# Four fused transformer layers on one core: wider products and another order in the MLPs

## What is computed

```python
h = norm(x)                                   # rmsnorm in L0, layer norm in L1, L2, L3
h = gelu(h @ w1 + b1) @ w2 + b2               # w1 (256, 1024), w2 (1024, 256)
x = x + h                                     # in L0 added to the layer's input
```

## Time and profile before

| | |
|---|---|
| median of three runs | 943.88 us |
| the profiled execution | 942.92 us |
| its span, first to last instruction | 941.1 us |
| instructions | 16083 |
| TensorE busy | 864.7 us (92%) |
| VectorE busy | 615.5 us (65%) |
| ScalarE busy | 486.8 us (52%) |
| GpSimd busy | 483.4 us (51%) |
| mean granted TensorE clock | 0.982 of 2.4 GHz |

### The profile page before, as it was taken

The page is one execution under the profiler, slowest core; times in us unless marked ns, Lnnn a source line. Parts: engine busy times, 40 slices in busy tenths (PEclk is TensorE's granted clock), DMA queues, the critical chain, the costliest instruction groups (busy, mean ns, idle before and its releaser), DMA issues.

```text
span 941.1 us, 16083 instructions
## 1 busy us (share of the span) xinstructions
PE 864.7 (92%) x5808; PEld 719.8 (76%) x5808; DVE 615.5 (65%) x1344; ACT 486.8 (52%) x1189; POOL 483.4 (51%) x508
## 2 busy tenths in 40 slices
PE   4788876899999999999899898999999999999898
PEld 3677755899976689767788686899966689766798
DVE  3788887426779767798442499417779757798340
ACT  2566655654753346632662344755753357533562
POOL 2767876474544245465385054464543345464383
PEclk8799999999999999999999999999999999999999
DMA  6833212002460014300000200202450024100001
GB/s 191 295 97 97 95 39 69 34 2 68 157 236 1 1 45 159 134 0 1 1 24 5 86 2 1 102 1 86 162 213 1 1 67 158 46 0 1 1 13 34
DMA packets 26674, 64.06 MB, mean 68 GB/s; under 512 B 2995, under 2 KB 15843, under 8 KB 25444
## 3 DMA queue, kind: packets, MB, share of 16 engines
q1 hardware_dynamic: 26596, 63.03, 20.2%
HBM read 57.22 MB, written 5.77 MB: 67 GB/s over the span
## 4 chain that ended last, share of the span: by engine, by line
PE 68%; DVE 20%; issue 5%; POOL 4%; ACT 1%; DMA 1%; SPq 1%; DVEq 0%; POOLq 0%
PE ps L960 7%; PE ps L900 6%; PE ps L859 6%; PE ps L861 6%; PE ps L889 5%; PE ps L936 4%; PE ps L758 3%; PE ps L701 3%; PE ps L702 3%; PE ps L703 3%; PE ps L682 3%; DVE prob L1640 3%; PE ps L683 3%; PE ps L684 3%; DVE mx L1639 3%
## 5 line engine op out<-in xcount | busy, mean ns | idle before, releaser
L960 PE MATMUL ps<-arena,pT_all 128*128 128x256 f32 x512 | 116.9, 382 | 5.8 <-DVE x L1660 3.7
L960 PEld LDWEIGHTS ps<-arena,pT_all 128*128 128x128 f32 x512 | 96.6, 191 | 32.3 <-issue 15.2
L936 PE MATMUL ps<-arena,hT 128*128 128x512 f32 x256 | 115.5, 594 | 0.0
L543 POOL TENSOR_TENSOR arena<-arena,rinv 128x640 f32<-128x640 f32 x64 | 80.3, 1256 | 53.4 <-DVE rinv L1454 53.3
L570 POOL TENSOR_TENSOR prob<-prob,rinv 128x512 f32<-128x512 f32 x32 | 49.5, 1547 | 113.3 <-DVE rinv L1653 113.3
L536 POOL TENSOR_TENSOR rstd<-var,neg_half 128x1 f32<-128x1 f32 (+1 forms) x56 | 33.9, 605 | 139.8 <-DVE var L1469 139.8
L1189 ACT ACTIVATE arena<-ps,nb 128x320 f32<-128x320 f32 x128 | 66.3, 523 | 56.7 <-DVE nb L1440 56.6
L1225 ACT ACTIVATE arena_r<-ps,cols 128x256 fp32r<-128x256 f32 x128 | 66.5, 520 | 54.2 <-PE ps L684 54.2
L512 POOL TENSOR_TENSOR vacc<-vacc,vpart 128x256 f32<-128x256 f32 x60 | 43.9, 732 | 98.6 <-ACT vpart L1297 98.4
L589 POOL TENSOR_TENSOR arena_r<-arena,arena_r 128x512 fp32r<-128x512 f32 x64 | 83.9, 1330 | 14.6 <-ACT arena L1226 14.6
L682 PE MATMUL ps<-hH,w1H 128*128 128x256 f32 x256 | 74.8, 292 | 11.9 <-DVE prob L1640 5.1
(11 more groups left out here) (166 smaller groups left out, 2325.2 us busy)
## 6 DMA issues: line engine op xcount, KB each, us to landing
ring<-in_heads_dram SPq DMA_DIRECT2D x64, 512.5 KB, 3.3
w<-in_w_dram SPq DMA_DIRECT2D x8, 1024.0 KB, 7.4
first_r<-spare_k SPq DMA_DIRECT2D x24, 160.0 KB
first_q<-spare_q SPq DMA_DIRECT2D x48, 64.0 KB, 2.4
spare_k<-HL SPq DMA_DIRECT2D x8, 320.0 KB, 2.4
spare_q<-HL SPq DMA_DIRECT2D x8, 256.0 KB, 2.5
x<-in_x_dram SPq DMA_DIRECT2D x1, 1024.0 KB, 6.0
lnb<-in_lnb_dram SPq DMA_DIRECT2D x4, 256.0 KB, 6.8
```

The source lines that it names most:

```text
L543: g.tensor_tensor(w, w, rinv[:, n % 2, 0:2].unsqueeze(2).broadcast_to([P, 2, KEYS0]), ALU.mult)\
L936: last = mm(ps[:, SCORES[k][half], :], hT[:, k, d, 0:P], A[:, d, b // 2, cols_of, sl, :].rearrange("p r s k -> p r (s k)"), start=(d == 0) ...
L960: last = mm(ps[:, 6, 0:D], pT[:, k, c, :], VW[:, b, c, :], start=(c == 0), stop=(c == PAIRS - 1))
```

## The change

1. The low and the high half of the second weight become slots 0 and 2 of one view, `w2_parts`; slot 1 is `w1H`, which lies between them. In `down` for batches 0 to 2 one product of 512 columns takes `hidH` against both halves, into both halves of a PSUM bank; low by high (256 columns) is added to the upper half. VectorE's `add` adds the two halves in two steps. Batch 3 keeps three products of 256.
2. Batches 2 and 3 are multiplied up together in `up_two`: 48 products of 512 columns, banks 0 to 3 in turn; gelu runs on 512 columns, GpSimd's subtraction on one f of both batches. In down 2 the low-by-high products stand behind all wide ones of the same tile.
3. Down uses banks 6 and 7 for even batches, 4 and 5 for odd ones; batches 2 and 3 are transposed into banks 4 and 5.
4. The order on TensorE is up 1, transposes of batch 3, down 0, down 1, `up_two`, down 2, (key products,) down 3. VectorE does spread 2, spread 3, z 2, z 3, split 2, split 3 and then the additions. GpSimd's two `power` steps stand ahead of the first rows.

```diff
-        w2L = overlay("w2L", [P, FT, D], F32R)
+        w2_parts = overlay("w2_parts", [P, 3, FT, D], F32R)
...
-        w2H = sb("w2H", [P, FT, D], F32R)
+        w2H_room = sb("w2H_room", [P, FT, D], F32R)
+        w2L, w2H = w2_parts[:, 0, :, :], w2_parts[:, 2, :, :]
...
         def turn_bank(l, b):
...
-            return TURN_M[l][b] if b < 2 else 4
+            return TURN_M[l][b] if b < 2 else b + 2
...
+        def ups_before(l, b):
+            return 3 * l * FT + min(b, 2) * FT
+        def down_banks(b):
+            return slice(6, 8) if b % 2 == 0 else slice(4, 6)
...
             def mlp_rows(l, name):
+                power(f"M{l}", 2, 2)
+                power(f"M{l}", 3, 2)
...
-                    if b + 2 < B:
-                        power(f"M{l}", b + 2, 2)
...
-                    for pair in range(FT // 2):
+                    if b == B - 1:
+                        for f in range(FT):
+                            pool.wait_ge(hid_ready, ups_before(l, 2) + f + 1)
+                            g.tensor_tensor(hidL[:, :, f, :], hid[:, :, f, :], hidH[:, :, f, :].bitcast(F32),
+                                            ALU.subtract).then_inc(hidL_ready, 1)
+                    for pair in range(FT // 2 if b < 2 else 0):
...
-                        pool.wait_ge(hid_ready, (l * B + b) * FT + 2 * pair + 2)
+                        pool.wait_ge(hid_ready, ups_before(l, b) + 2 * pair + 2)
...
-                        pe.wait_ge(hid_ready, (n - 1) * FT + f + 2)
+                        pe.wait_ge(hid_ready, ups_before(l, b - 1) + f + 2)
...
-                    if f == FT // 2 - 1 and 1 <= b < B - 1:
-                        turn_m(l, b + 1)
+                    if f == FT // 2 - 1 and b == 1:
+                        turn_m(l, 2)
+            def up_two(l):
+                pe.wait_ge(hs_ready, l * B + 4)
+                for f in range(FT):
+                    if f >= 4:
+                        pe.wait_ge(hid_ready, ups_before(l, 2) + f - 3)
+                    block = slice(f * P, (f + 1) * P)
+                    o = ps[:, f % 4, :].rearrange("p (k n) -> p k n", k=2)
+                    for d in range(DH):
+                        mm(o, w1H[:, d, block], hH[:, :, d, :], start=(d == 0), stop=False)
+                        mm(o, w1H[:, d, block], hL[:, :, d, :], start=False, stop=False)
+                        last = mm(o, w1L[:, d, block], hH[:, :, d, :], start=False, stop=(d == 1))
+                    last.then_inc(f1_ps, 1)
...
             def down(l, b):
-                n, k = l * B + b, b % 2
+                k = b % 2
...
+                elif b == 1:
+                    pe.wait_ge(hm_ready, l * B + 4)
...
-                    pe.wait_ge(rows_done, rows_before(f"M{l}") + b)
+                    pe.wait_ge(rows_done, rows_before(f"M{l}") + b - 1)
...
+                    o = ps[:, down_banks(b), :][:, u, :]
+                    low = hidL[:, 1 - k if b < 2 else k, :, at]
...
-                        if u == 0 and f % 2 == 0:
-                            pe.wait_ge(hidL_ready, (n * FT + f) // 2 + 1)
-                        o = ps[:, 5 + u, 0:D]
-                        mm(o, hidH[:, k, f, at], w2H[:, f, :], start=(f == 0), stop=False)
-                        mm(o, hidH[:, k, f, at], w2L[:, f, :], start=False, stop=False)
-                        last = mm(o, hidL[:, 1 - k, f, at], w2H[:, f, :], start=False, stop=(f == FT - 1))
+                        if u == 0 and b == 2:
+                            pe.wait_ge(hid_ready, ups_before(l, 2) + f + 1)
+                        elif u == 0 and b < 2 and f % 2 == 0:
+                            pe.wait_ge(hidL_ready, 16 * l + 4 * b + f // 2 + 1)
+                        if b < B - 1:
+                            mm(o.rearrange("p (c n) -> p c n", c=2), hidH[:, k, f, at], w2_parts[:, 0:3:2, f, :],
+                               start=(f == 0), stop=False)
+                            if b < 2:
+                                last = mm(o[:, D:2 * D], low[:, f, :], w2H[:, f, :], start=False, stop=(f == FT - 1))
+                        else:
+                            mm(o[:, 0:D], hidH[:, k, f, at], w2H[:, f, :], start=(f == 0), stop=False)
+                            mm(o[:, 0:D], hidH[:, k, f, at], w2L[:, f, :], start=False, stop=False)
+                            last = mm(o[:, 0:D], low[:, f, :], w2H[:, f, :], start=False, stop=(f == FT - 1))
+                    if b == 2:
+                        for f in range(FT):
+                            if u == 0:
+                                pe.wait_ge(hidL_ready, 16 * l + 8 + f + 1)
+                            last = mm(o[:, D:2 * D], low[:, f, :], w2H[:, f, :], start=False, stop=(f == FT - 1))
...
             def attend0():
...
             def mlp(l):
-                base = l * B
-                for i in range(1, B + 1):
-                    if i == 1 and l == 2:
-                        up(l, i, range(0, 6))
-                        pe.wait_ge(rows_done, rows_before(f"M{l}"))
-                        up(l, i, range(6, FT))
-                    elif i < B:
-                        up(l, i, range(FT))
-                    elif l % 2 == 0:
-                        pe.wait_ge(hid_ready, (base + B - 1) * FT + 4)
-                        heads_kv(l, 0)
-                        heads_kv(l, 1)
-                    if i == 1:
-                        pe.wait_ge(rows_done, rows_before(f"M{l}"))
-                    down(l, i - 1)
+                up(l, 1, range(0, 6))
+                if l == 2:
+                    pe.wait_ge(rows_done, rows_before(f"M{l}"))
+                up(l, 1, range(6, FT))
+                pe.wait_ge(rows_done, rows_before(f"M{l}"))
+                turn_m(l, 3)
+                down(l, 0)
+                down(l, 1)
+                up_two(l)
+                down(l, 2)
+                if l % 2 == 0:
+                    heads_kv(l, 0)
+                    heads_kv(l, 1)
+                down(l, 3)
...
             def gelus(l, b, fs):
...
-                n = l * B + b
...
-                        act.wait_ge(f1_ps, n * FT + f + 2)
+                        act.wait_ge(f1_ps, ups_before(l, b) + f + 2)
...
-                    if f == FT // 2 - 1 and 1 <= b < B - 1:
-                        turned_m(l, b + 1)
+                    if f == FT // 2 - 1 and b == 1:
+                        turned_m(l, 2)
...
             def mlp(l):
-                for b in range(1, B):
-                    if b >= 2:
-                        act.wait_ge(f2_ps, l * B + b - 1)
-                    gelus(l, b, range(FT))
+                _, _, bias, gelu = MLP[l]
+                gelus(l, 1, range(FT))
+                turned_m(l, 3)
+                for f in range(FT):
+                    act.wait_ge(f1_ps, ups_before(l, 2) + f + 1)
+                    o = ps[:, f % 4, :].rearrange("p (k n) -> p k n", k=2)
+                    a_(hidH[:, :, f, :], o, gelu, bias=col(bias, f))
+                    a_(hid[:, :, f, :], o, gelu, bias=col(bias, f)).then_inc(hid_ready, 1)
...
             def keys(a, seq):
...
-                    v.tensor_tensor(x[:, 2 * b:2 * b + 2, :], ps[:, 5:7, 0:D], x[:, 2 * b:2 * b + 2, :], ALU.add)\
-                        .then_inc(rows_done, 1)
+                    rows = x[:, 2 * b:2 * b + 2, :]
+                    if b < B - 1:
+                        link(v.tensor_tensor(rows, ps[:, down_banks(b), 0:D], rows, ALU.add))
+                        v.tensor_tensor(rows, ps[:, down_banks(b), D:2 * D], rows, ALU.add).then_inc(rows_done, 1)
+                    else:
+                        v.tensor_tensor(rows, ps[:, down_banks(b), 0:D], rows, ALU.add).then_inc(rows_done, 1)
...
-                for b in range(B):
-                    if b == 0:
-                        dve.wait_ge(rows_done, rows_before(f"M{l}"))
-                    if b + 2 < B:
-                        mlp_spread(l, b + 2)
-                        mlp_z(l, b + 2)
-                    if b >= 1:
-                        if b + 1 < B:
-                            mlp_split(l, b + 1)
-                        add(b - 1)
+                dve.wait_ge(rows_done, rows_before(f"M{l}"))
+                mlp_spread(l, 2)
+                mlp_spread(l, 3)
+                mlp_z(l, 2)
+                mlp_z(l, 3)
+                mlp_split(l, 2)
+                mlp_split(l, 3)
+                for b in range(B - 1):
+                    add(b)
```

## The result

The changed kernel took 950.59 us (median of 5 runs, 944.71 to 953.87), the kernel before, beside it, 944.42 (942.02 to 945.03): ratio 1.0059, 95% interval 1.0039 to 1.0080. Slower, then, by more than the 0.3% bound; the forecast was 946.3 and no difference the likeliest case. The median lies 0.1 us above the range of 941.0 to 950.5. The range was drawn from a kernel before at 943.88 us, and as a ratio its upper end is 1.0070, so by the ratio the result lies inside. The profiled execution took 950.95 us; its span is 949.2, 8.1 more than before's.

What follows compares the result with a forecast made beforehand. TensorE bounds the kernel, with GpSimd's queue becoming the bound in down 0 and 1. Merging gives about -3.3 us, waits +5.8: +2.5, so the profiled 942.92 becomes 945.4 and the median 946.3; range 941.0 to 950.5.

Steps and rivals of the forecast that it cites:

- GpSimd's queue: In down 0 and down 1: becomes the bound, ending down 1 at 619.6 instead of 617.15 in MLP 2.
- The stalls there: TensorE waiting for GpSimd's low halves in down 0 and above all down 1, some 2.4 us per MLP.
- The banks' gain: In MLP 1 and 3, down 3 no longer waits for VectorE to empty the banks: 1.05 us in all.
- The second addition: On VectorE after batches 0 to 2: 0.7 us more, free because its readers leave 2 us of room.
- part 1: Fewer, wider products in up_two and the downs: 96 merges per MLP saving 13 ns each; about -3.3 us given back.
- rival A: The forecast itself: wide products 225 ns apart, both splits disturb GpSimd's subtractions; +2.5 us, 946.3; chance 0.50.
- rival C: Slow side: the excess grows with the columns, wide products 238 ns apart, merging saves nothing; +3.3, 949.6; chance 0.18.
- the end of down 2: Last low half ready 2.7 us after up_two, then 0.12 and 2.74: MLP 2's down 2 ends at 636.0, 1.3 later.
- Rivals B: Weight load costs the 12 ns and 512 columns cover it, so products 215.6 ns apart; -2.6 us, 943.7; chance 0.20.
- B2: 215.6 ns spacing, and the splits fall beside the products, so four subtractions take 5.08 us, not 5.54; 939.9; chance 0.12.

Runs made afterwards that it cites:

- banks_only: The kernel before, with down(l, 3) of MLP 1 and 3 writing banks 2 and 3 instead of down 2's banks; 941.00 us, ratio 0.9966.
- wide_old_order: The kernel before, with only the wide products in down of batches 0 to 2 and two additions, order and banks unchanged; 945.62 us, ratio 1.0014.
- late_swap: rows_late with the 16 wide products of down(l, 2) ahead of its 16 low-half products; 939.53 us, ratio 0.9951.
- after_again: The changed kernel run once more with no edit; 948.97 us, ratio 1.0060 against the kernel before.
- late_adjacent: rows_late with both parts of the second weight side by side, so a wide product reads 512 contiguous columns; 939.60 us, ratio 0.9950.
- split_late: The changed kernel, with VectorE's splits of batches 2 and 3 waiting until GpSimd's eight subtractions are done; 945.63 us, ratio 1.0012.
- rows_late: The changed kernel, with GpSimd's row additions moved behind its subtractions of batches 0 and 1; 937.74 us, ratio 0.9941.

## Why the prediction was right in its mechanism and too low in its size

**Where it was right.** GpSimd's queue is the bound of down 0 and down 1, for the reasons given. In us after the start of MLP 2, forecast and measured: row additions of batch 0 done 5.14, 5.24; its low halves 10.64, 10.71; those of batch 1 17.54, 17.52; end of down 1 21.04, 21.21. The stalls there are 2.48 us (13.86 against 11.38 without them) where 2.4 stood; 1.3 of them lie in down 0 and 1.2 in down 1, not above all in down 1. `up_two` took 10.89 us for 10.85, and neither ScalarE nor GpSimd held it. The banks' gain was put at 1.05 us and banks_only gives 1.03. The second addition hides in the new order, as was said; wide_old_order shows what it costs where its 2 us of room aren't there.

**Step that was mis-sized: part 1, the merges in a down.** The 225 ns of rival A hold in `up_two`:
```profile
626.72 0.39 PE L712 MATMUL ps<-hH,w1H 128*128 128x512 f32 x1
626.95 0.39 PE L713 MATMUL ps<-hL,w1H 128*128 128x512 f32 x1
627.18 0.39 PE L714 MATMUL ps<-hH,w1L 128*128 128x512 f32 x1
```
226 to 227 ns apart, against 240 for two of 256. In the downs it is otherwise, here in down 0:
```profile
616.74 0.39 PE L735 MATMUL ps<-w_parts,arena_r 128*128 128x512 f32 x1
616.97 0.28 PE L738 MATMUL ps<-w_parts,arena_r 128*128 128x256 f32 x1
617.09 0.40 PE L735 MATMUL ps<-w_parts,arena_r 128*128 128x512 f32 x1
617.33 0.28 PE L738 MATMUL ps<-w_parts,arena_r 128*128 128x256 f32 x1
```
A wide product and the one behind it stand 229 to 240 ns apart there, 233 on average: with the narrow one behind it a pair takes 353 to 355 ns, three narrow ones took 354. That is close to rival C's price (238), in half of the places, while the other half went A's way. The forecast took one price for all fp32r products; the earlier trace rows could have warned it, since the 13 ns came from one row of another stage. The merges gave back 2.94 us, of 3.3 forecast: 2.3 in `up_two` (2.5 forecast), 0.6 in the downs (0.8 forecast). So this step accounts for 0.4 of the 2.0 us by which the MLPs missed.

The rule of the Trainium skill ("TensorE: Matmul & The Clock Gate", section "Wait — 56ns, not 53.3ns?") puts products N / 2.4 + 2.5 ns apart, 216 ns at 512 columns. The fp32r products here don't follow it, neither at 256 columns (118 and 120 ns) nor at 512 (227 and 233). Worked out from it, a merge is worth 2.5 ns (an estimate from the Trainium skill's figures); the downs gave 3 ns each (0.58 us for 192 merges), but from other spacings than the rule's.

**Step that was mis-sized: the end of down 2.** 5.91 us instead of 5.55, the largest part of the miss. The first half takes 3.11 us instead of 2.82: the last subtraction ends 2.83 us after `up_two` rather than 2.7 (GpSimd's eight take 10.81 us together, since it follows ScalarE, one per 1.36 us), and from there to the second half it is 0.28 us where 0.12 was taken, as the product starts 0.05 after the subtraction and takes 0.1 longer than one in a row. The prediction gave that 0.1 to the bank wait of the earlier trace rows and forgot it at GpSimd's stalls. The eight wide products of the second half add 0.05. late_swap hides the wait, and takes 0.31 us off each MLP.

**The sum.** Forecast and measured per MLP: +0.6 and +1.07, +0.3 and +0.79, +1.3 and +1.86, +0.3 and +0.81; together +2.5 and +4.53. In MLP 2 the missing 0.57 us are 0.17 at the end of down 1 (0.08 from the eight wide products of its second half, 0.1 from the product after the last stall), 0.04 in `up_two` and 0.36 in down 2, and the other three miss by about the same 0.5, as they have the same chain.

**What was left out.** All outside the MLPs was taken as unchanged, and so was the clock. 3.5 of the 5.6 us between 945.4 and the profiled 950.95 are of that kind, and by after_again (0.979 on average in both kernels) no part of the change. It would also explain why five runs gave +6.2 us where the work accounts for 4.6; the clocks of before's five runs are not on record, so that is not shown. A term for it belonged in the range: the times given for before, 942.02 to 944.42, already held 2.4 us of it.

**The verdict.** "Same" got 0.48 and "slower" 0.40. With +4.5 in place of +2.5 it would have been clearly slower, as rival C's sum (949.6) was, which names the wrong share of products but the right side. Rivals B and B2 fall with the 227 ns (they need 215.6).

## What to carry to other kernels

When stages are put next to each other, take the queue of every engine that feeds them, lay its instructions out in order, and ask for each whether the waiting engine needs it now: here moving eight row additions behind the subtractions turned a loss of 4.5 us in the MLPs into a gain of 4.8. Price an instruction in the stage in which it will stand, with the operands it will read there; the same merge was worth 13 ns in one place and 3 on average in another. Count what a stall costs beyond its wait, here 0.1 us each. And when a kernel's runs spread with the clock, compare kernels by stage lengths from the trace as well as by medians, as the work saved and the clock granted can point in opposite directions.

## What the runs showed of the hardware

- fp32r products of 512 columns stand 226.5 ns apart in `up_two` (213.3 of stream and 13 more, the same 13 as at 256 columns), but 229 to 240 in the downs. That is not due to the order of stages (wide_old_order has it), a gap in the operand (late_adjacent) or adding into the same bank (late_swap). What it is due to stays open; moving and stationary operands are other tiles there. The tiles alone don't settle it: in the kernels with late rows, down 0 and 1 of MLP 0 have 229 to 230 ns nearly throughout (mean 229.3 to 229.5 in five traces), while the same instructions in MLP 1 to 3 have 229 and 240 in turn (mean 234.2 to 234.5).
- Two engines side by side: a VectorE split of 512 columns takes 0.68 us alone and up to 1.78 beside GpSimd's subtraction, which itself grows from 1.28 to as much as 1.78 us. With the splits moved away (split_late) every subtraction takes 1.28 to 1.35 us again; the splits, now beside row additions in MLP 2, take 1.20 and 1.22, and those additions 1.19 instead of 0.73.
- The granted clock is not the same from run to run nor from kernel to kernel: 0.969 to 0.987 in runs of these kernels, 0.60 us for each 0.001. rows_late had 0.982 on average in 18 runs on two occasions, late_swap 0.976 in 24, though they differ only in the order of the 32 products of down 2 in each MLP. Why is open.
